# A Flamingo-style block on one core: the first half of batch 0 in two quarters of 256 tokens, with 25 split pieces of W0 held on chip

## The chip, the core and the metric

The kernel runs on one core of one Trainium2 chip. The metric is device time in microseconds (us), from the program's first instruction to its last with the launch around it, as a median of several runs. Five engines work side by side and meet through semaphores: TensorE (PE, matrix products and transposes), VectorE (DVE), ScalarE (ACT), GpSimd (POOL) and SyncE (SP), which issues most of the transfers between DRAM and the on-chip memory. Each engine takes its instructions strictly in the order of the program, so an instruction that waits holds back everything behind it on its engine.

## The reference

The input x has 4 batches of 1024 tokens with 1024 channels; ctx_2048, of the same shape, is the value v.

```
x = x + tanh(g_xattn) * wkv(w, u, k = layernorm(x), v = ctx_2048)
x = x + tanh(g_ffn)   * ffn(layernorm(x))

wkv: along the tokens, for each channel:  y = (p + e^(u+k) v) / (q + e^(u+k))
     p = e^w p + e^k v ;  q = e^w q + e^k        (written with running maxima)
ffn: D = gelu(f16(x) @ W0.T + b0) -> f16   (4096 columns)
     E = D @ W1.T + b1            -> f16   (1024 columns)
```

## The kernel before

**Work.** W0 and W1 are kept as two f16 parts (hi and lo), so each product is done twice and accumulated. W0 comes in 32 pieces of 128 rows. For a piece, `hi_piece` (ACT, two passes over 128x1024) writes the hi part and the scaled f32 piece, and `lo_piece` (POOL) writes the lo part; `store_piece` puts both into DRAM, from where later halves and batches read them back as blocks of four pieces (`load_parts`). All this is done once, in batch 0.

**Slots.** PE's main loop counts slots: a slot is one group of 16 products of 128 columns of weights with 512 tokens (8 blocks of channels, hi and lo). Per batch there are 64 slots of the first layer (`group1`, 32 pieces for each half of 512 tokens), then 64 of the second (`quarter2`). In batch 0 the first half of the tokens takes slots 0 to 31, and the second half 32 to 63. Each group accumulates in one of three banks (`BANKS`), which ACT empties with a Gelu (`gelu`); a group may start when the Gelu of three groups earlier is done.

**The front.** What a half needs before its first group is called the front here. For tiles of 128 tokens: the first layernorm (`stats_x`, `norm_x`, `lessen_x`: DVE and ACT, rstd on POOL), then, for each of 8 blocks of 128 channels, a *unit*: PE transposes the block (`unit`), ACT takes its exponential (`exps`), DVE runs seven operations (a product with v, two scans along the tokens, two fused operations, a reciprocal and a last fused one), and POOL adds the result to x (`residual`) and then sets the scan seeds of the unit after the next (`seed`). After all 8 units PE transposes back to tokens (`tokens_x2`), DVE does the second layernorm (`stats_x2`, `norm_x2`), PE transposes to channels (`channels_x2`) and ACT copies into XT (`copy_xt`), which is the moving operand of the first layer. The same steps serve the second half of batch 0; for batches 1 to 3 another form is used (`keys`, `means`, `variances`), which the change leaves as it is.

**Order.** The front of the first half stands ahead of the slots. All else is placed in the slots by hand: `UNIT_SLOT` says in which slot a unit starts, `LN1_SLOT` and `LN2_SLOT` do the same for the two layernorms. Exponentials and Gelus use different tables of ACT, so each unit inside the first layer's slots costs two table loads. In the fronts of batch 0 the units of the second half stand in slots 5 to 22, its second layernorm in slots 27 to 32, one tile per slot, and the 24 remaining pieces of W0 are split in slots 0 to 23.

Of the kernel before, what the change touches and what calls it, by code (L numbers as in the profile page):

```python
# [6 lines left out]
ALU = mybir.AluOpType  # L7
# [4 lines left out]
P = 128  # L12
# [19 lines left out]

UNIT_SLOT = {}
LN1_SLOT = {}
LN2_SLOT = {}
MEAN_SLOT = {}
VAR_AFTER, DEV_AFTER, SCALE_AFTER = 6, 8, 11
KEY_SLOT = {}


def place_front():
    for i, k in enumerate((5, 6, 9, 12, 14, 17, 20, 22)):
        UNIT_SLOT[CB + i] = k
    for i, k in enumerate((40, 43, 47, 50, 54, 57, 61, 64, 68, 71, 75, 78, 82, 85, 89, 92)):
        UNIT_SLOT[UNITS + i] = k
    for i in range(HT):
        LN1_SLOT[HT + i] = 1 + i
        LN1_SLOT[2 * HT + i] = 26 + 2 * i
        LN1_SLOT[3 * HT + i] = 52 + 2 * i
        LN2_SLOT[HT + i] = (27 + i, 29 + i)  # L50
    for h in range(2):
        MEAN_SLOT[2 + h] = 98 + 13 * h
    for i in range(HT):
        LN1_SLOT[2 * TILES + i] = 112 + 2 * i
    for b in (1, 2):
        at, n, T = SLOTS * b, UNITS * (b + 1), TILES * (b + 1)
# [8 lines left out]
    for n in range(UNITS, UNITS * B):  # L65
        KEY_SLOT[n] = UNIT_SLOT[n] - 2 if n % UNITS == 0 else UNIT_SLOT[n - 1]


place_front()
UNITS_AT = {k: [n for n in UNIT_SLOT if UNIT_SLOT[n] == k] for k in set(UNIT_SLOT.values())}  # L70
KEYS_AT = {k: [n for n in KEY_SLOT if KEY_SLOT[n] == k] for k in set(KEY_SLOT.values())}
LN1_AT = {k: T for T, k in LN1_SLOT.items()}
X2T_AT = {k[0]: T for T, k in LN2_SLOT.items()}
X2_AT = {k[1]: T for T, k in LN2_SLOT.items()}
# [6 lines left out]

def group_of(b, k):

    if k < GROUPS1:
        return GROUPS * b + k
    return GROUPS * b + GROUPS1 + (k - GROUPS1) // Q if k % Q == Q - 1 else None
# [10 lines left out]
def build(nc, x, xT, vT, consts, wrow, w0, w1, out):  # L97
# [6 lines left out]
    with ExitStack() as ctx:  # L104
# [35 lines left out]
        squares = xh[:, :].bitcast(F32)  # L140
        tokens = sb("tokens", [P, 2, HT])

        V = sb("V", [P, 2, HALF])
        S = sb("S", [P, 2, 2, HALF + 1])
# [8 lines left out]
        xo = sb("xo", [P, 2, L])  # L153
        ring = [stage[:, i, :] for i in range(RING2)] + [xo[:, i, :] for i in range(2)]
# [8 lines left out]
        x_landed, v_landed, xT_landed = sems("x_landed", HT), sems("v_landed"), sems("xT_landed", 8)  # L163
        x2_stored, xo_landed, out_stored = sems("x2_stored"), sems("xo_landed"), sems("out_stored")
        wst_landed, w_landed, w_stored = sems("wst_landed", RING1), sems("w_landed"), sems("w_stored")
# [19 lines left out]
        def unit_banks(n):  # L185

            pair = front[n % 2]
            return pair[:, 0, :], pair[:, 1, :]

        def token_banks(T):  # L190

            if T in (0, 3):
                return accs[:, 0:2, :]
            return front[(T + 1) % 2 if T < HT else T % 2][:, :, :]

        def last_stage_of(b):
            return GROUPS * (b + 1)
# [7 lines left out]
        def _(sp):  # L205
            def load_x(T):
                half, slot = T // HT, T % HT if T < TILES else T % 2
                if 0 < half < 4:
                    sp.wait_ge(kt_done, CB * min(half, 2))
# [9 lines left out]
            def load_norms(half):  # L219
# [3 lines left out]
                if half >= 4:  # L223
                    sp.wait_ge(k_ready, CB * (half - 3))
                row = norms_dram[half:half + 1].rearrange("o a p k -> o (a p k)")
                sp.dma_start(xin[:, 2 + half % 2, :], row.to_broadcast([P, 2 * HALF])).then_inc(norms_landed[half % 2], 16)

            def load_v(n):
                if n >= 2:
                    sp.wait_ge(ev_done, n - 1)  # L230
                sp.dma_start(V[:, n % 2, :], vT[n // UNITS, n % UNITS]).then_inc(v_landed[n % 2], 16)

            def load_xT(n):
                b, i = divmod(n, UNITS)
                if n >= 8:
                    sp.wait_ge(x2_done, n - 7)
                if b:

                    if b == 1:
                        sp.wait_ge(x2t_done, HT * (i // CB + 1))  # L240
                    else:
                        sp.wait_ge(scaled, UNITS * (b - 2) + CB * (i // CB + 1))
# [771 lines left out]
```

## Time and profile before

| what | us |
|---|---|
| median of 3 runs (1917.05 to 1918.54) | 1918.29 |
| the profiled execution | 1916.53 |
| its span, first to last instruction | 1914.7 |
| PE busy in the span | 1812.3 |
| DVE, ACT, POOL busy | 879.1, 555.7, 333.9 |

The span is what the trace shows; the profiled execution's time is 1.83 us longer than its span. PE busy counts from the start of a product to its modelled end. All stretches below are us from the span's start.

### The profile page before, as it was taken

The numbers are of one execution on the slowest core, as the hardware profiler recorded it, in microseconds if no ns is written. First come the engines' busy times: TensorE is split into PE (matmuls) and PEld (weight loads), VectorE is DVE, ScalarE is ACT, GpSimd is POOL, SyncE is SP. The second block draws the span as 40 slices with busy tenths as digits, with TensorE's granted clock in tenths as the row PEclk, the third lists the DMA queues.
The fourth block names the chain that finished last, engine by engine and source line by source line (L and its number), as shares of the span: only waits on it lengthen the run. The fifth ranks groups of instructions, "written<-read, shape, count | busy, mean of one in ns | idle before, by whom it ended". The sixth has DMA issues, their size and how long they took to land.

```text
span 1914.7 us, 20205 instructions
## 1 busy us (share of the span) xinstructions
PE 1812.3 (95%) x8408; PEld 829.5 (43%) x8408; DVE 879.1 (46%) x997; ACT 555.7 (29%) x673; POOL 333.9 (17%) x325
## 2 busy tenths in 40 slices
PE   1189899999999999999999999999999999999999
PEld 0144444444444444444444444444444444444444
DVE  8968748898447857633215867742300000000000
ACT  5059534634424434311003434410101221100000
POOL 4336402565211211200001221200000000000000
PEclk9999999999999999999999999999999999999999
DMA  6639776767574443332452443233233212222330
GB/s 247 247 118 327 236 259 232 251 238 267 195 213 143 146 151 133 141 108 104 138 185 106 149 160 137 89 132 128 93 120 132 88 45 88 88 81 95 132 121 34
DMA packets 82953, 291.89 MB, mean 152 GB/s; under 512 B 12583, under 2 KB 12583, under 8 KB 75693
## 3 DMA queue, kind: packets, MB, share of 16 engines
q1 hardware_dynamic: 74940, 177.30, 27.3%
q10 hardware_dynamic: 7920, 113.30, 16.8%
q8 instruction: 66, 1.08, 0.2%
q14 instruction: 27, 0.21, 0.0%
HBM read 223.41 MB, written 67.16 MB: 152 GB/s over the span
## 4 chain that ended last, share of the span: by engine, by line
PE 90%; DVE 1%; ACT 1%; DMA 1%; POOL 1%; issue 1%; SPq 0%; ACTq 0%; DVEq 0%; POOLq 0%
PE accs L903 45%; PE accs L925 44%; POOL W L447 0%; DVE stats L626 0%; DMA var_dram<-tokens 0%; ACT W L555 0%; PE front L861 0%; PE back L870 0%; DMA total<-var_dram 0%; PE front L884 0%; DVE XT L757 0%; PE front L879 0%; DVE xh L673 0%; DMA var_dram<-total 0%; PE front L837 0%
## 5 line engine op out<-in xcount | busy, mean ns | idle before, releaser
L903 PE MATMUL accs<-XT,W 128*128 128x512 f16 x4096 | 888.9, 379 | 4.2 <-ACT XT L527 2.4
L925 PE MATMUL accs<-DT,W 128*128 128x512 f16 x4096 | 886.7, 379 | 0.0
L925 PEld LDWEIGHTS accs<-DT,W 128*128 128x128 f16 x4096 | 400.8, 98 | 487.3 <-issue 6.8
L903 PEld LDWEIGHTS accs<-XT,W 128*128 128x128 f16 x4096 | 400.8, 98 | 486.3 <-issue 5.1
L765 DVE SCALAR_TENSOR_TENSOR xo<-e,tg,xo 128x512 f32<-128x512 f16 x64 | 50.3, 787 | 633.0 <-ACT e L572 633.0
L564 ACT ACTIVATE DT<-accs,small 128x512 f16<-128x512 f32 x256 | 175.6, 686 | 516.0 <-PE accs L903 515.4
L572 ACT ACTIVATE e<-accs,small 128x512 f16<-128x512 f32 x64 | 43.9, 686 | 660.3 <-PE accs L925 660.3
L720 DVE RECIPROCAL S<-front 128x512 f32<-128x512 f32 x64 | 214.4, 3350 | 0.0
L425 POOL TENSOR_TENSOR X<-X,S 128x512 f32<-128x512 f32 x64 | 92.5, 1446 | 521.1 <-DVE S L723 521.1
L447 POOL TENSOR_TENSOR W<-stage,W 128x1024 f16<-128x1024 f32 x52 | 110.6, 2138 | 46.3 <-ACT stage L558 46.3
L706 DVE TENSOR_TENSOR front<-front,V 128x512 f32<-128x512 f32 x64 | 44.5, 696 | 137.6 <-ACT front L522 136.0
L708 DVE TENSOR_TENSOR_SCAN S<-decay,S,front 128x512 f32<-128x512 f32 x64 | 81.3, 1271 | 0.0
L711 DVE TENSOR_TENSOR_SCAN S<-decay,S,front 128x512 f32<-128x512 f32 x64 | 80.4, 1256 | 0.0
L837 PE MATMUL front<-ident,xin 128*128 128x128 f32 x64 | 14.3, 355 | 61.6 <-DVE S L723 42.5
L555 ACT ACTIVATE W<-stage 128x1024 f16<-128x1024 f32 x52 | 54.5, 1048 | 46.3 <-DMA stage<-w_in 46.3
L757 DVE TENSOR_TENSOR XT<-X,total 128x512 f16<-128x512 f32 x48 | 30.0, 686 | 73.2 <-DMA total<-var_dram 73.2
L564 ACT ACT_TABLE_LOAD x49 | 62.9, 1283 | 0.9
L522 ACT ACT_TABLE_LOAD x48 | 61.6, 1283 | 0.8
L694 DVE TENSOR_TENSOR front<-X,xin 128x512 f32<-128x512 f32 x48 | 40.7, 847 | 42.0 <-DMA xin<-norms_dram 41.1
L558 ACT ACTIVATE stage<-stage 128x1024 f32<-128x1024 f32 x52 | 55.0, 1057 | 1.6
L522 ACT ACTIVATE front<-front,shift 128x512 f32<-128x512 f32 x64 | 42.3, 660 | 40.8 <-PE front L837 31.5
L723 DVE SCALAR_TENSOR_TENSOR S<-front,tg,S 128x512 f32<-128x512 f32 x64 | 48.1, 752 | 7.0 <-DVE S L720 0.5
(69 smaller groups left out, 596.1 us busy)
## 6 DMA issues: line engine op xcount, KB each, us to landing
W<-parts_dram ACTq DMA_DIRECT2D x54, 2048.0 KB, 9.2
parts_dram<-W SPq DMA_DIRECT2D x64, 512.0 KB, 5.1
stage<-w_in SPq DMA_DIRECT2D x52, 512.0 KB, 5.7
xin<-x_in SPq DMA_DIRECT2D x32, 512.0 KB, 7.0
V<-vT_in SPq DMA_DIRECT2D x64, 256.0 KB, 5.5
X<-xT_in SPq DMA_DIRECT2D x64, 256.0 KB, 6.6
x_dram<-X SPq DMA_DIRECT2D x32, 512.0 KB, 4.5
xo<-x_dram SPq DMA_DIRECT2D x32, 512.0 KB, 4.3
```

Of the source, the lines that this page charges most:

```text
L425: nc.gpsimd.tensor_tensor(slot, slot, S[:, n % 2, 1, 0:HALF], ALU.add).then_inc(x2_done, 1)
L447: nc.gpsimd.tensor_tensor(W[:, (g // Q) % 2, 1, g % Q, :], ring[ring_slot(g)[0]], W[:, (g // Q) % 2, 0, g % Q, :], ALU.subtract).then_inc( ...
L522: nc.scalar.activation(bank, bank, ACT.Exp, bias=shift[:, half, n % CB:n % CB + 1]).then_inc(e_ready, 1)
L555: nc.scalar.activation(W[:, s % 2, 0, g % Q, :], ring[slot], ACT.Copy, scale=W_SCALE)\
L558: nc.scalar.activation(ring[slot], ring[slot], ACT.Copy, scale=W_SCALE).then_inc(ws_done, 1)
L564: nc.scalar.activation(DT[:, nb, HALF * half:HALF * (half + 1)], acc[m % BANKS], ACT.Gelu, bias=b0[:, nb:nb + 1], scale=1.0 / W_SCALE).the ...
L708: nc.vector.tensor_tensor_scan(S_q[:, 1:], decay[:, c:c + 1].to_broadcast([P, HALF]), E, S_q[:, 0:1], ALU.mult, ALU.add).then_inc(q_done, 1)
L711: nc.vector.tensor_tensor_scan(S_p[:, 1:], decay[:, c:c + 1].to_broadcast([P, HALF]), EV, S_p[:, 0:1], ALU.mult, ALU.add).then_inc(p_done, 1)
L720: nc.vector.reciprocal(S_q[:, 0:HALF], E).then_inc(rec_done, 1)
L765: nc.vector.scalar_tensor_tensor(o, e16[:, half, :], tg[:, 1:2], o, ALU.mult, ALU.add)\
L903: mm = nc.tensor.matmul(acc[m % BANKS], W[:, (nb // Q) % 2, part, nb % Q, P * c:P * (c + 1)], XT[:, c, HALF * half:HALF * (half + 1)], sta ...
L925: mm = nc.tensor.matmul(acc[m % BANKS], W[:, s % 2, part, q, P * c:P * (c + 1)], DT[:, nb, HALF * half:HALF * (half + 1)], start=(nb == 0 ...
```

## The change

The first half of batch 0 is no longer prepared as 512 tokens, but as two quarters of 256. The front of the first quarter (8 units of 256 tokens, two tiles) stands ahead of the slots. Then follow 64 *early* groups of 16 products with 256 tokens (`group_early`, in the order of the table `EARLY`), two for each of the 32 pieces, so that the slots of batch 0 count 32 more (`EXTRA`). In early slots 0 to 24 (`LAG` = 25) the first quarter meets pieces 0 to 24, while the units of the second quarter run (in slots 1, 3, 8 and 13, two at a time). At slot 25 (`SECOND`) the second quarter's second layernorm and the first layernorm of the second half stand, with no group between them. From there the second quarter meets all pieces and the first quarter the last seven, while the second half's units (512 tokens) run from slot 31 to 61. At slot 64 (`THIRD`) the second half's second layernorm stands for all four tiles, again with no group between, and then slot 32 of the old count follows, unchanged.

Both quarters need each piece, so pieces 0 to 24 stay on chip until the second quarter has used them: `piece` places them in parts of X2, XT, DT and W that are not yet in use. 15 pieces are split ahead of the slots instead of 8, 10 more in early slots 1 to 19, the last seven in slots 34 to 52. Stores to DRAM start at early slot 3, each as two transfers. The second layernorm writes to two buffers in turn (`xhs`) instead of one. The units of batch 1 stand in slots 43 to 92 instead of 40 to 92 of the old count.

```diff
+LAG = 25
+EARLY = ([(0, nb) for nb in range(LAG)] + [(1, nb) for nb in range(12)] +
+         [x for j in range(NB - LAG) for x in ((0, LAG + j), (1, 12 + 2 * j), (1, 13 + 2 * j))] +
+         [(1, nb) for nb in range(12 + 2 * (NB - LAG), NB)])
+EXTRA = len(EARLY) - NB
...
+SECOND, THIRD = LAG, len(EARLY)
...
-    for i, k in enumerate((5, 6, 9, 12, 14, 17, 20, 22)):
-        UNIT_SLOT[CB + i] = k
+    for i, (k, a) in enumerate(((1, 5), (1, 8), (3, 10), (3, 13), (8, 16), (8, 19), (13, 21), (13, 24))):
+        UNIT_SLOT[CB + i], ADD_SLOT[CB + i] = k, a
+    for i, (k, a) in enumerate(((31, 36), (32, 41), (37, 46), (42, 50), (47, 55), (51, 60), (56, 63), (61, 63))):
+        UNIT_SLOT[2 * CB + i], ADD_SLOT[2 * CB + i] = k, a
...
+WITH_UNIT = ((0, 1), (2,), (3, 4), (5,), (6, 7), (8,), (9, 10), (11,))
+BEHIND = (12, 13, 14)
+PREP_SLOT = {15 + j: 1 + 2 * j for j in range(LAG - 15)}
+PREP_SLOT.update({LAG + j: 34 + 3 * j for j in range(NB - LAG)})
...
+            def group_early(m):
+
+                quarter, nb = EARLY[m]
+                pe.wait_ge(lo_done, nb + 1)
+                if m >= BANKS:
+                    pe.wait_ge(acc_drained, m - BANKS + 1)
+                for c in range(CB):
+                    for part in range(2):
+                        mm = nc.tensor.matmul(acc[m % BANKS][:, 0:QUARTER], piece_block(nb, part, c),
+                                              XT[:, c, QUARTER * quarter:QUARTER * (quarter + 1)],
+                                              start=(c == 0 and part == 0), stop=(c == CB - 1 and part == 1))
+                mm.then_inc(mm_done, 1)
...
-            for T in range(HT):
-                copy_xt(T)
+            hi_piece(BEHIND[0])
+            norm_x(2)
+            copy_xt(0)
+            copy_xt(1)
+            norm_x(3)
+            for g in BEHIND[1:]:
+                hi_piece(g)
...
+                    if K == SECOND:
+                        tokens_x2(2)
+                        tokens_x2(3)
+                        channels_x2(2)
+                        channels_x2(3)
+                    if K == THIRD:
+                        tokens_x2(4)
+                        for T in range(4, 8):
+                            if T < 7:
+                                tokens_x2(T + 1)
+                            channels_x2(T)
```

The names in the rows below leave out buffer numbers (front, X for X2); `xN` is the number of instructions that a row stands for. On PE, from the last transposes of the first front on, the order before was this (L903 the groups of 512 tokens, L837 a unit's transposes):

```order
L861 MATMUL accs<-ident,X 128x128 x8
L870 MATMUL back<-ident,xh 128x128 x16
L903 MATMUL accs<-XT,W 128x512 x80
L837 MATMUL front<-ident,xin 128x128 x4
L903 MATMUL accs<-XT,W 128x512 x16
L837 MATMUL front<-ident,xin 128x128 x4
L903 MATMUL accs<-XT,W 128x512 x48
```

and at the same place it is now this (L1083 the groups of 256 tokens, L1019 the transposes of two units):

```order
L1058 MATMUL back<-ident,xh 128x128 x8
L1058 MATMUL back<-ident,total 128x128 x8
L1083 MATMUL accs<-XT,X 128x256 x16
L1019 MATMUL front<-ident,xin 128x128 x4
L1083 MATMUL accs<-XT,X 128x256 x32
L1019 MATMUL front<-ident,xin 128x128 x4
L1083 MATMUL accs<-XT,X 128x256 x16
```

The groups begin after two tiles instead of four, and the next units' transposes stand one group behind the first instead of five. On ACT, the order from there on was this before (L527 the copies to XT, L564 Gelus and their table, L555 and L558 the two passes of a piece):

```order
L527 ACTIVATE XT<-back 128x8x128 x4
L564 ACT_TABLE_LOAD
L564 ACTIVATE DT<-accs,small 128x512
L555 ACTIVATE W<-xo 128x1024
L558 ACTIVATE xo<-xo 128x1024
L564 ACTIVATE DT<-accs,small 128x512
```

and is this now (L662 the copies, L638 a tile of the first layernorm, L694 and L696 a piece, L704 Gelus, L653 exponentials):

```order
L662 ACTIVATE XT<-back 128x8x128 x2
L638 ACTIVATE xin<-xin,offset,rstd 128x1024
L694 ACTIVATE W<-xo 128x1024
L696 ACTIVATE xo<-xo 128x1024
L694 ACTIVATE W<-xo 128x1024
L696 ACTIVATE xo<-xo 128x1024
L704 ACT_TABLE_LOAD
L704 ACTIVATE DT<-accs,small 128x256
L653 ACT_TABLE_LOAD
L653 ACTIVATE front<-front,shift 128x256 x2
L704 ACT_TABLE_LOAD
L704 ACTIVATE DT<-accs,small 128x256
```

A tile, two pieces, three table loads and a Gelu now stand between the last copy and the second Gelu, with the second quarter's first two exponentials among them. On POOL, at the first residuals in the slots, the order was this before (L447 `lo_piece`, L425 `residual`, L410 `seed`):

```order
L447 TENSOR_TENSOR W<-stage,W 128x1024 x3
L447 TENSOR_TENSOR W<-xo,W 128x1024 x2
L425 TENSOR_TENSOR X<-X,S 128x512
L410 COPY S<-state 128x2
L447 TENSOR_TENSOR W<-stage,W 128x1024
L425 TENSOR_TENSOR X<-X,S 128x512
L410 COPY S<-state 128x2
```

and is this now (L568 `lo_piece`, L544 `residual`, L528 `seed`):

```order
L568 TENSOR_TENSOR DT<-stage,DT 128x2x512
L544 TENSOR_TENSOR X<-X,S 128x256
L559 COPY state<-S 128x2
L528 COPY S<-state 128x2
L568 TENSOR_TENSOR DT<-stage,DT 128x2x512
L568 TENSOR_TENSOR DT<-xo,DT 128x2x512
L544 TENSOR_TENSOR X<-X,S 128x256
L559 COPY state<-S 128x2
L528 COPY S<-state 128x2
```

A residual, and the seed behind it, stands behind one or two pieces, as before, but the unit that waits for the seed is now half as long.

## Rows read from the trace of the kernel before

**Rows 1.** Busy time (instructions) by engine in three stretches; then clock, DMA, GB/s.

```profile
0.00:112.13 112.13, 22.05 (x96) 14.41 (x97) 93.64 (x113) 32.08 (x37) 37.41 (x55) 0.98 0.59 211
112.13:240.16 128.03, 121.95 (x608) 59.24 (x609) 100.99 (x112) 99.33 (x109) 70.01 (x53) 0.99 0.75 256
240.16:1914.70 1674.54, 1668.34 (x7704) 755.87 (x7704) 684.42 (x774) 424.34 (x528) 226.49 (x218) 1.00 0.41 141
```

**Rows 2.** Timeline, first front: start, length, engine, line [idle before].

```profile
14.37 0.69 PE L837 MATMUL front<-ident,xin 128*128 128x128 f32 x2 [2.19 <-DVE xin L660]
...
21.09 0.69 PE L837 MATMUL front<-ident,xin 128*128 128x128 f32 x2 [2.56 <-DVE xin L660]
...
22.39 0.70 DVE L706 TENSOR_TENSOR front<-front,V 128x512 f32<-128x512 f32 x1 [1.36 <-ACT front L522]
...
30.78 0.69 DVE L706 TENSOR_TENSOR front<-front,V 128x512 f32<-128x512 f32 x1
...
88.78 0.75 DVE L723 SCALAR_TENSOR_TENSOR S<-front,tg,S 128x512 f32<-128x512 f32 x1
```

**Rows 3.** Groups by line, shapes apart: busy us, mean ns, idle before; DVE, units.

```profile
L720 DVE RECIPROCAL S<-front 128x512 f32<-128x512 f32 x64 | 214.4, 3350 | 0.0
...
L708 DVE TENSOR_TENSOR_SCAN S<-decay,S,front 128x512 f32<-128x512 f32 x64 | 81.3, 1271 | 0.0
...
L723 DVE SCALAR_TENSOR_TENSOR S<-front,tg,S 128x512 f32<-128x512 f32 x64 | 48.1, 752 | 7.0 <-DVE S L720 0.5
...
L781 DVE SCALAR_TENSOR_TENSOR shift<-wp,shift 128x8 f32<-128x8 f32 x1 | 0.2, 168 | 0.0
```

**Rows 4.** Timeline, second layernorm of the first half, to the first group.

```profile
91.44 1.30 DVE L626 BATCH_NORM_STATS2 stats<-accs 128x6 f32<-128x512 f32 x2 [1.91 <-PE accs L944]
...
93.15 1.30 DVE L626 BATCH_NORM_STATS2 stats<-front 128x6 f32<-128x512 f32 x2
...
94.79 1.34 DVE L673 TENSOR_SCALAR xh<-accs,mv,rstd 128x1024 f16<-128x1024 f32 x1
...
96.18 1.03 PE L870 MATMUL back<-ident,xh 128*128 128x128 f16 x8 [3.08 <-DVE xh L673]
...
97.01 1.91 PE L861 MATMUL front<-ident,X 128*128 128x128 f32 x8
97.25 1.02 ACT L527 ACTIVATE XT<-back 128x1024 f16<-128x1024 f16 x1 [22.61 <-PE back L870]
...
112.13 1.46 PE L903 MATMUL accs<-XT,W 128*128 128x512 f16 x3 [1.11 <-ACT XT L527]
```

**Rows 5.** Groups by line, shapes apart: ACT and POOL.

```profile
L564 ACT ACTIVATE DT<-accs,small 128x512 f16<-128x512 f32 x256 | 175.6, 686 | 516.0 <-PE accs L903 515.4
L447 POOL TENSOR_TENSOR W<-stage,W 128x1024 f16<-128x1024 f32 x52 | 110.6, 2138 | 46.3 <-ACT stage L558 46.3
...
L564 ACT ACT_TABLE_LOAD x49 | 62.9, 1283 | 0.9
...
L555 ACT ACTIVATE W<-stage 128x1024 f16<-128x1024 f32 x52 | 54.5, 1048 | 46.3 <-DMA stage<-w_in 46.3
...
L522 ACT ACTIVATE front<-front,shift 128x512 f32<-128x512 f32 x64 | 42.3, 660 | 40.8 <-PE front L837 31.5 <-DVE front L698 8.8
```

**Rows 6.** Busy time in three short stretches, columns as in Rows 1.

```profile
113.00:114.00 1.00, 1.00 (x4) 0.42 (x3) 0.93 (x4) 0.38 (x1) 0.70 (x1) 0.50 0.00 0
116.00:117.00 1.00, 1.00 (x7) 0.43 (x5) 0.93 (x4) 0.00 (x0) 0.00 (x0) 1.00 0.00 0
200.00:206.00 6.00, 4.63 (x22) 1.89 (x20) 5.75 (x5) 5.91 (x8) 5.02 (x4) 1.00 0.51 197
```

**Rows 7.** Timeline, the end of the second half's last unit.

```profile
211.85 0.75 DVE L723 SCALAR_TENSOR_TENSOR S<-front,tg,S 128x512 f32<-128x512 f32 x1
```

**Rows 8.** The chain that ended last, from slot 32 on: start, length, what.

```profile
240.16 110.68 PE accs L903 x512
```

**Rows 9.** Busy time in a stretch of batch 1's units, columns as in Rows 1.

```profile
350.00:380.00 30.00, 30.00 (x140) 13.58 (x139) 20.70 (x20) 16.28 (x18) 19.63 (x15) 1.00 0.93 330
```

More of the change, by code:

```diff
@@ new lines, in _ @@
+            for g in BEHIND:
+                load_piece(g + RING1)
+            for b in range(B):
+                for k in range(0 if b else -EXTRA, SLOTS):
+                    K = EXTRA + SLOTS * b + k
+                    if K - 1 in PREP_AT and PREP_AT[K - 1] + RING1 < NB:
+                        load_piece(PREP_AT[K - 1] + RING1)
+                    if K in STORE_AT:
+                        store_piece(STORE_AT[K])
+                    if b == 0:
+                        if k == NB - Q + 1:
+                            for g in range(Q):
+                                stored(sp, g)
+                                stored(sp, LAG + g)
+                            load_parts(0, AT[1, LAG + Q - 1] + 1)
@@ L423, in residual @@
                 pool.wait_ge(xT_landed[n % 8], 16 * (n // 8 + 1))
-                slot = X2[:, n % UNITS, :]
-                nc.gpsimd.tensor_tensor(slot, slot, S[:, n % 2, 1, 0:HALF], ALU.add).then_inc(x2_done, 1)
-                half, c = n // CB, n % CB
-                if n >= UNITS and c:
+                b, h, off, w, c = chunk(n)
+                slot = X2[:, CB * h + c, off:off + w]
+                nc.gpsimd.tensor_tensor(slot, slot, S[:, n % 2, 1, 0:w], ALU.add).then_inc(x2_done, 1)
+                half = 2 * b + h
+                if n >= FIRST and c:
                     pool.wait_ge(x2_done, n + 1)
@@ L573, in round_e @@
                                      bias=b1[:, g // 2:g // 2 + 1], scale=1.0 / W_SCALE).then_inc(acc_drained, 1)
-            for T in range(HT):
+            for T in range(2):
                 norm_x(T)
@@ L783, in _ @@
             offset_x(0)
-            for T in range(HT):
-                if T + 1 < HT:
-                    stats_x(T + 1)
-                lessen_x(T)
-                if T + 1 < HT:
-                    offset_x(T + 1)
+            stats_x(1)
+            lessen_x(0)
+            offset_x(1)
+            lessen_x(1)
             dve.wait_ge(s_act0, 3)
@@ L857, in tokens_x2 @@
-                pe.wait_ge(y_done, UNITS * b + (UNITS if b else CB * (h + 1)))
-                if T >= 2:
-                    pe.wait_ge(xh_ready, T - 1)
+                ready = (2 if T < HT else 3) * CB
+                pe.wait_ge(x2_done, ready)
+                pe.wait_ge(y_done, ready)
+                pe.wait_ge(xh_ready, T - 1)
                 for c in range(CB):
-                    mm = nc.tensor.transpose(rows[:, c // HT, P * (c % HT):P * (c % HT + 1)],
-                                             X2[:, CB * h + c, P * (tile % HT):P * (tile % HT + 1)], ident[:, :])
+                    mm = token_piece(T, c)
```

522 lines of the change are left out of this document (320 added, 202 removed).

## The prediction

> **What bounds the kernel now.** The first view to read is busy time by stretch [rows 1]. From 240.16 to the end PE is busy 1668 of 1675 us: nothing can be won there except by fewer products, and the change has as many as before. From 112.13 to 240.16, the 32 slots of the first half, PE is busy 122 of 128. Before 112.13 it is busy 22, all of it transposes, while DVE is busy 94: the first front is one chain on DVE. So the time to win is the 112 us before the first group and the 6 us after. Whatever the change does is settled when slot 32 starts, at 240.16 [rows 8]; what follows keeps its 1674.5 us if nothing later is disturbed. I therefore work out when slot 32 starts.
>
> The timeline of the first front [rows 2] shows the first unit on DVE from 22.39, the second from 30.78, 8.39 later, and the eighth ending at 88.78 + 0.75 = 89.53: eight units without a gap. The second layernorm then takes 22.6 to the first group at 112.13 [rows 4]. In the second half the last unit ends at 211.85 + 0.75 = 212.60 [rows 7], and slot 32 comes 27.6 later.
>
> **The change, step by step.** Times are us from the span's start.
>
> *First unit.* Its transposes wait for tile 1 instead of tile 3: 14.37 instead of 21.09 [rows 2]. The exponential and DVE follow as before, 1.30 later, less about 0.25 for half the columns: 15.4 (before 22.39).
>
> *Eight units of 256 tokens.* Halving 8.39 gives 4.19, the lower bound. Seven operations each keep half of a fixed part; an operation on 8 columns takes 0.168, so the upper bound is 4.19 + 7 × 0.084 = 4.78. The longest, reciprocal (3.35) and scans (1.27) [rows 3], are nearly all columns, and neighbours overlap a little; I take 4.51. Eight units: 36.1, to 51.5 (before 89.53). ACT splits 1.5 pieces a unit, 1.5 × 2 × 1.05 = 3.1 plus the exponential [rows 5], and POOL 1.5 × 2.14 = 3.2 plus the residual: both fit below 4.51, so I add nothing; if loads of pieces come late, this cover is gone and up to 5 us are lost.
>
> *Second layernorm of two tiles.* DVE does three statistics of 1.64 (93.15 to 94.79), a normalization of 1.34, another statistic and normalization: 9.2, and 0.3 until POOL's last residual; then transposes 1.03 and copy 1.02, gaps 0.2 [rows 4]. The sum, 11.8, puts the first group at 63.3 (before 112.13): 48.8 won so far.
>
> *Slots 0 to 24.* PE: a group of 512 tokens takes 110.68/512 × 16 = 3.46 [rows 8], one of 256 between 1.73 and 1.75, since a product takes 216.2 ns where its columns at 2.4 GHz take 213.3; 25 groups are 43.8. The 32 transposes of units cost 2.4 (half of the 1.91 for eight, which were slow) [rows 4]. At the first group PE's granted clock was 0.50, that is 1.2 GHz, and it was 1.00 by 116 [rows 6]: 1.7 lost. Together 47.9.
> ACT: the rest of the first layernorm, one pass (about 1.2); twelve pieces of 2.1 (two for `BEHIND`, ten in the slots); nine table loads of 1.283; 25 Gelus and 8 exponentials of 256 columns. Those lie between half of 0.686 and all of it; by the difference between passes of 1024 (1.05) and 512 columns (0.66) [rows 5] a half-width one takes 0.47, and 0.40 with the overlap of neighbours. Sum: 1.2 + 25.2 + 11.5 + 13.2 = 51.1, with bounds 49.2 and 60.7. So ACT, not PE, sets this stretch. It ends the last piece before its last five Gelus, at 63.3 + 49.1 = 112.4, and PE has then about 5.9 of groups to go: 118.3.
> DVE: the second quarter's first exponential stands behind the pass, two pieces, two table loads, a Gelu and itself: 63.3 + 8.8 = 72.1. Eight units would end at 108.2. But each unit's scan needs a seed, which POOL writes behind the residual two units earlier, behind pieces that wait for ACT. For unit 10: piece 16 leaves ACT at 82.5 and POOL 2.14 later, residual and seed take 1.0, so 85.6, where DVE is ready at 81.5: it waits 4.1. The same sum for the next units gives 1 to 3 each and 9.4 in all: 117.6, and 118.4 with the last residual. Both chains meet at 118.3; I take that.
>
> *Slot 25.* PE has nothing but transposes until XT is there: eight transposes 0.95, two statistics 3.3, normalization 1.34, a first-layernorm pass taken at 0.8 (between half and all of that normalization, which has the same size), statistic 1.64, normalization 1.34, transposes and copy 2.05, less some overlap: 11.2. It is 129.5. Before, no such hole was there: the first half had one front.
>
> *To the second half's units.* Six groups (10.5) hide the rest of the first layernorm on DVE. Then Gelu, table load, exponential: 0.40 + 1.28 + 0.66 + 0.1. PE's clock may have fallen in the hole; I add half of 1.7. The first unit starts at 143.3. Eight units at 8.39, DVE-bound: 67.1, to 210.4. PE comes to the units' slots one to three us after the bank is free, and ACT needs three more, inside the 8.39; before, ACT was busy 99 of 128 in slots 0 to 31 [rows 1] with 24 pieces among them; here seven stand in this stretch.
>
> *Slot 64.* From the last unit to the first statistic 1.91 passed before (89.53 to 91.44), with one transpose left; now eight are left, 1.67 more. Four tiles then took 20.7 to the first group (91.44 to 112.13) [rows 4]; the second buffer takes out one wait, 0.45. So 210.4 + 3.6 + 20.2 = 234.2, and the clock has fallen again: 1.7 more, 235.9. Before, five groups of PE lay beside this chain; here none is left to put there.
>
> *Afterwards.* Batch 1's units begin three slots (10.4) later and end in the same slot. DVE idled 9.3 in 350 to 380 alone [rows 9], which takes up most of it: 0, at worst some 5. Transfers: SP issues each store as two and starts them later, behind waits for pieces; DMA was busy 0.75 of the time in slots 0 to 31 and 0.59 before [rows 1], and the same bytes are spread over the same stretch: 0. What stands behind those waits on SP are the loads of v for the second quarter's last units; they are issued some 8 us before their unit, which covers them.
>
> **Sum.** Slot 32 moves from 240.16 to 235.9: 4.3 won, out of 48.8 won at the first group. The span becomes 1910.4, the profiled execution (1.83 above its span) 1912.2, and the median, which was 1.76 above the profiled execution, **1914.0**.
>
> **Rivals.** A difference of 0.2%, 3.8 us, is about what can be told from no change here.
> (a) *Forecast*, 1914.0, own range 1910 to 1918: chance 0.46.
> (b) *The waits are not there.* If Gelus stay near their lower bound and POOL's pieces come in time, slots 0 to 24 end with PE, at 63.3 + 47.9 = 111.2, 7.1 earlier; units of 4.19 give 2.6 more: 1904.3. For it: both chains have bounds that low. Against it: the piece, table loads and Gelus on ACT are in strict order. Chance 0.19.
> (c) *All is given back*: the change brings the first group forward, but not slot 32. Gelus of 0.55 instead of 0.40 add 0.15 × 33 = 5.0 to ACT's stretch: 1919. For it: 48.8 won and 44.5 lost are both sums of estimates, so their difference can vanish. Chance 0.16.
> (d) *Slower, by the seeds.* The units of the second quarter wait for POOL, POOL for ACT's pieces, ACT for PE's groups between them. If the six gated units wait twice what I found, 18.8 instead of 9.4, slot 25 comes 9.4 later: 1923.4. It decides from 17.5 us of waits on. For it: ACT was busy 5.9 of 6 us at 200 to 206, where PE had gaps [rows 6], so such a loop exists. Against it: pieces come on ACT every 4 us, and a unit takes 4.5. Chance 0.12.
> (e) *Slower, by the clock.* If the gaps between groups in slots 0 to 24 take the clock to 1.2 GHz, 25 groups take 86.5 instead of 43.8, and with the transposes the stretch ends at 154.6, 36.3 later: 1950. Against it: from 200 to 206 PE was busy 4.63 of 6 and the granted clock stayed 1.00 [rows 6]; I expect 43.8 + 2.4 of 55 busy, about that share. Chance 0.07.
> The Trainium skill, "TensorE: Matmul & The Clock Gate", section "A second HAM failure mode: psum-queue depth-cycling", speaks for (e): it tells of a kernel that went round its PSUM banks and idled briefly between groups, so that its clock fell and rose again and again. By that rule the result would be somewhere between (a) and (e); no row here shows it yet.
>
> **The numbers.** The likeliest is (a), 1914.0. The range reaches down to (b) and up past (d), **1903 to 1925**; outside lie (e) and the tails of (b) and (d). Faster by over 0.2% (below 1914.5): all of (b) and over two thirds of (a), 0.52. Within 0.2%: the rest of (a) and most of (c), 0.28. Slower: (d), (e) and the tail of (c), 0.20.
>
> **What would show it.** In the changed kernel's profile: the first unit on DVE at 15.4, and eight in 36; the first group at 63 with the clock at 0.50; PE in gaps up to slot 18, released by ACT's Gelus, and DVE's scans waiting for seeds; slot 25's hole of 11 from about 118; the second half's first unit at 143 and eight in 67 without waits; slot 64's hole from the last unit's end near 210 for 24 us; slot 32's groups from 234 to 236. The prediction is wrong if slots 0 to 24 take under 50 or over 62 us, if the second half's units wait for ACT or PE, or if PE waits at batch 1's means.

## The result, and the profile after

The changed kernel takes **1929.11 us** (median of 7 runs, 1924.20 to 1931.39), the kernel before 1918.29 (7 runs, 1917.05 to 1919.52). The ratio is 1.0051, 95% interval 1.0038 to 1.0064: slower by half a per cent, clear of its interval, where 1914.0 was forecast. The profiled execution took 1929.11, its span 1927.3.

Busy time by stretch, columns as in [rows 1]. The second and the fourth row are the groups of 256 tokens, the third and the fifth the two pauses between fronts, the last begins at slot 32:

```profile
0.00:64.14 64.14, 13.05 (x49) 6.18 (x49) 55.12 (x95) 36.84 (x43) 40.14 (x57) 1.00 0.68 234
64.14:119.60 55.46, 48.33 (x416) 41.06 (x416) 38.36 (x59) 49.81 (x67) 31.53 (x33) 1.00 0.78 253
119.60:132.31 12.71, 4.03 (x32) 3.27 (x33) 12.07 (x23) 2.51 (x3) 3.17 (x7) 0.73 1.04 395
132.31:215.40 83.09, 74.77 (x656) 64.68 (x656) 69.54 (x66) 56.66 (x77) 27.16 (x23) 0.98 0.64 216
215.40:244.53 29.13, 10.79 (x64) 9.18 (x65) 19.61 (x30) 4.57 (x5) 4.19 (x7) 0.60 0.37 149
244.53:1927.30 1682.77, 1673.48 (x7704) 757.05 (x7704) 687.47 (x785) 424.48 (x528) 228.81 (x222) 1.00 0.41 140
```

The first group starts at 64.14 (before 112.13 [rows 4]), but slot 32 at 244.53 (before 240.16 [rows 8]), and the rest takes 1682.8, 8.2 more than before [rows 1]. So 4.4 us are lost ahead of slot 32 and 8.2 behind it. What is new stands in column PEclk, the granted clock (third from the right): 0.73 and 0.60 in the pauses. Its 1.00 in the first row is no reading, since this trace's first record of the clock is at 67.4. The transposes just ahead of the first group, and that group itself, ran at half clock: eight transposes took 1.03, where run 10 has 0.61 at full clock, and 16 products 3.48, where a later group took 1.91.

```profile
59.12 1.03 PE L1058 MATMUL back<-ident,xh 128*128 128x128 f16 x8 [4.62 <-DVE xh L831]
...
64.14 3.48 PE L1083 MATMUL accs<-XT,X 128*128 128x256 f16 x16 [1.12 <-ACT XT L662]
...
82.10 1.91 PE L1083 MATMUL accs<-XT,DT 128*128 128x256 f16 x16 [2.00 <-ACT DT L704]
```

```profile
118.95 0.61 PE L1060 MATMUL back<-ident,xh 128*128 128x128 f16 x8
```

VectorE's timeline (start, length, then in brackets the idle time ahead and what ended it): the first unit of each front, the unit of the second half that waits longest, and the last unit's last operation.

```profile
73.60 0.43 DVE L870 TENSOR_TENSOR front<-front,V 128x256 f32<-128x256 f32 x1 [6.40 <-ACT front L653]
...
147.16 0.70 DVE L870 TENSOR_TENSOR front<-front,V 128x512 f32<-128x512 f32 x1 [5.68 <-ACT front L653]
...
184.97 0.70 DVE L870 TENSOR_TENSOR front<-front,V 128x512 f32<-128x512 f32 x1 [3.94 <-ACT front L653]
...
219.99 0.75 DVE L887 SCALAR_TENSOR_TENSOR S<-front,tg,S 128x512 f32<-128x512 f32 x1
```

The second half's eight units take 147.16 to 220.74, 73.6, where eight without a wait take 67.1. Whom TensorE waited for between the pauses (total in us, times, longest):

```profile
PE accs L1083 <- POOL W L568: 8.0, 7, 1.9
PE accs L1083 <- ACT XT L662: 1.1, 1, 1.1
PE accs L1083 <- ACT DT L704: 0.3, 1, 0.3
```

Seven waits, one for the lower part of each of the pieces 25 to 31. TensorE's timeline behind the second pause:

```profile
244.53 112.52 PE L1102 MATMUL accs<-XT,W 128*128 128x512 f16 x512 [1.12 <-ACT XT L662]
356.89 117.58 PE L1124 MATMUL accs<-DT,W 128*128 128x512 f16 x544
476.45 1.53 PE L1067 MATMUL front<-total,share 128*128 128x512 f32 x2 [1.99 <-DVE S L887]
477.77 22.18 PE L1124 MATMUL accs<-DT,W 128*128 128x512 f16 x96
...
549.25 2.08 PE L1072 MATMUL front<-xh,share 128*128 128x512 f32 x2 [2.68 <-DVE xh L908]
```

Slot 32's 512 products take 112.52 (before 110.68 [rows 8]), the means of batch 1 wait 1.99 for its last unit, and the 96 products behind them take 22.18; the same count at the second means, further on, takes 20.88. From 477 to 480 the granted clock was 0.50. Why batch 1 comes late stands in VectorE's and ScalarE's rows:

```profile
281.16 0.76 DVE L857 SCALAR_TENSOR_TENSOR front<-grow,wp,front 128x512 f32<-128x512 f32 x1
287.33 0.70 DVE L870 TENSOR_TENSOR front<-front,V 128x512 f32<-128x512 f32 x1 [5.42 <-ACT front L653]
...
285.27 1.28 ACT L653 ACT_TABLE_LOAD   x1
286.57 0.66 ACT L653 ACTIVATE front<-front,shift 128x512 f32<-128x512 f32 x1
...
368.33 1.06 ACT L694 ACTIVATE W<-stage 128x1024 f16<-128x1024 f32 x1 [4.52 <-DMA stage<-w_in]
```

VectorE has its keys at 281.92 and waits for the exponential of the first unit, which stands in slot 43.

### The profile page after: what moved, and what is told of

Its sections match the earlier page's. It is cut to its first block, busy times and chain, and to the rows that moved or that the text cites. A ratio compares the mean times of both kernels' runs of the same rounds, so it can differ in the third digit from the quotient of the medians.

```text
span 1927.3 us, 21556 instructions
## 1 busy us (share of the span) xinstructions
PE 1824.5 (95%) x8920; PEld 881.4 (46%) x8920; DVE 882.2 (46%) x1053; ACT 574.9 (30%) x721; POOL 335.0 (17%) x349
## 4 chain that ended last, share of the span: by engine, by line
PE 77%; DVE 11%; ACT 4%; issue 4%; POOL 3%; DMA 1%; SPq 0%; DVEq 0%; POOLq 0%; ACTq 0%
PE accs L1124 38%; PE accs L1102 36%; DVE S L884 3%; PE accs L1083 1%; POOL W L568 1%; DVE S L872 1%; DVE S L875 1%; DVE stats L784 1%; POOL X L544 1%; DVE front L870 1%; ACT L653 1%; DVE front L853 1%; DVE front L881 1%; DVE front L878 1%; ACT L704 1%
## 5 line engine op out<-in xcount | busy, mean ns | idle before, releaser
L1102 PE MATMUL accs<-XT,W 128*128 128x512 f16 x3584 | 776.0, 380 | 1.1 <-ACT XT L662 1.1
L712 ACT ACTIVATE DT<-accs,small 128x512 f16<-128x512 f32 x224 | 154.0, 688 | 490.9 <-PE accs L1102 490.4
L884 DVE RECIPROCAL S<-front 128x512 f32<-128x512 f32 (+1 forms) x72 | 215.6, 2994 | 0.0
L544 POOL TENSOR_TENSOR X<-X,S 128x512 f32<-128x512 f32 (+1 forms) x72 | 94.0, 1305 | 492.6 <-DVE S L887 492.6
L870 DVE TENSOR_TENSOR front<-front,V 128x512 f32<-128x512 f32 (+1 forms) x72 | 45.8, 636 | 135.1 <-ACT front L653 135.1
L568 POOL TENSOR_TENSOR W<-stage,W 128x1024 f16<-128x1024 f32 x41 | 86.7, 2128 | 60.3 <-ACT stage L696 60.3
L872 DVE TENSOR_TENSOR_SCAN S<-decay,S,front 128x512 f32<-128x512 f32 (+1 forms) x72 | 83.0, 1153 | 8.7 <-POOL S L528 8.7
L875 DVE TENSOR_TENSOR_SCAN S<-decay,S,front 128x512 f32<-128x512 f32 (+1 forms) x72 | 81.9, 1138 | 0.0
L1083 PE MATMUL accs<-XT,W 128*128 128x256 f16 x480 | 54.9, 273 | 9.8 <-POOL W L568 8.0
L694 ACT ACTIVATE W<-stage 128x1024 f16<-128x1024 f32 x41 | 43.0, 1048 | 51.6 <-DMA stage<-w_in 51.6
L696 ACT ACTIVATE stage<-stage 128x1024 f32<-128x1024 f32 x52 | 55.0, 1057 | 1.6
L784 DVE BATCH_NORM_STATS2 stats<-xin 128x6 f32<-128x512 f32 x64 | 41.0, 683 | 30.3 <-DMA xin<-x_in 30.3
L1083 PEld LDWEIGHTS accs<-XT,W 128*128 128x128 f16 x480 | 46.3, 98 | 17.4 <-POOL W L568 9.8
L887 DVE SCALAR_TENSOR_TENSOR S<-front,tg,S 128x512 f32<-128x512 f32 (+1 forms) x72 | 49.8, 692 | 7.5
```

What stands on the lines that cost most here:

```text
L544: nc.gpsimd.tensor_tensor(slot, slot, S[:, n % 2, 1, 0:w], ALU.add).then_inc(x2_done, 1)
L568: nc.gpsimd.tensor_tensor(lo, staged, hi, ALU.subtract).then_inc(lo_done, 1)
L712: nc.scalar.activation(DT[:, nb, HALF * half:HALF * (half + 1)], acc[m % BANKS], ACT.Gelu, bias=b0[:, nb:nb + 1], scale=1.0 / W_SCALE).the ...
L784: nc.vector.bn_stats(stats[:, i, h, :], halves[h]).then_inc(bn_done[i], 1)
L870: nc.vector.tensor_tensor(EV, E, values, ALU.mult).then_inc(ev_done, 1)
L872: nc.vector.tensor_tensor_scan(S_q[:, 1:w + 1], decay[:, c:c + 1].to_broadcast([P, w]), E, S_q[:, 0:1], ALU.mult, ALU.add).then_inc(q_done, 1)
```

## The experiments

Medians are given with the ratio to the kernel before, run beside it on the same chip; differences between kernels are differences of these ratios times 1918.3 us. All versions lie within 1% of the kernel before, so where two intervals meet, a difference rests on the traces as well. Edits are to the changed kernel unless another run is named; `...` stands for code that is not shown.

**1. The last seven pieces earlier.**

```
-PREP_SLOT.update({LAG + j: 34 + 3 * j for j in range(NB - LAG)})
+PREP_SLOT.update({LAG + j: 33 + 2 * j for j in range(NB - LAG)})
```

> Only the slots of ScalarE's and GpSimd's work on the last seven pieces of W0 (25 to 31) move: 33, 35, 37, ... in place of 34, 37, 40, ... so three to nine groups stand between a piece's slot and its use, in place of two. Theory (the pieces' loop): between the Gelu of a piece's slot and its first use ScalarE needs 1.05 and 1.06 us and GpSimd 2.12 us, more than the two groups of 1.75 us behind which they are hidden, so TensorE waits for nearly every piece (8.0 us in all), the exps behind its stalled stream come late, and VectorE's units lose 6 us (waits of 3.94, 1.28, 0.70 and 0.16). Expected: these waits are gone, the last unit ends near 214 in place of 220.7, slot 32 starts near 238 in place of 244.5, and the kernel takes 6 to 7 us less than the changed kernel, about 1922.6, still slower than before. Rival (the stretch is VectorE's and ScalarE's own: the 3.94 comes from table loads and queues on ScalarE): TensorE's wait on GpSimd goes but the units' end stays within 2 us, and the time stays within 2 us of 1929.

1921.79, ratio 1.0017 (1.0008 to 1.0026): 6.5 us less than the changed kernel. The loop stands in the changed kernel's timelines, here ScalarE's, GpSimd's and TensorE's rows for one piece:

```profile
166.93 0.48 ACT L704 ACTIVATE DT<-accs,small 128x256 f16<-128x256 f32 x1 [3.38 <-PE accs L1083]
167.31 1.05 ACT L694 ACTIVATE W<-stage 128x1024 f16<-128x1024 f32 x1
168.38 1.06 ACT L696 ACTIVATE stage<-stage 128x1024 f32<-128x1024 f32 x1
...
169.52 2.13 POOL L568 TENSOR_TENSOR W<-stage,W 128x1024 f16<-128x1024 f32 x1 [4.60 <-ACT stage L696]
...
171.70 1.92 PE L1083 MATMUL accs<-XT,W 128*128 128x256 f16 x16 [0.88 <-POOL W L568]
```

The Gelu waits for TensorE, the piece's halves for the Gelu, GpSimd for them, and TensorE for GpSimd: 4.8 us round, with two groups (3.5) to cover it. With the edit one wait of 0.4 is left of the 8.0, and VectorE waits for ScalarE once in place of four times:

```profile
PE accs L1083 <- POOL W L568: 0.4, 1, 0.4
...
DVE front L870 <- ACT front L653: 6.6, 1, 6.6
```

The units take 148.57 to 216.34, 67.8, and slot 32 comes at 240.13 (expected 238: the first unit came 1.4 later than in the changed kernel). The theory holds. Of the 7.1 between the two profiled executions, 4.4 lie ahead of slot 32 and 2.7 behind it, where TensorE's wait at the second variances is 1.39 instead of 2.68 and the clock does not fall after it.

**2. The seeds earlier.**

```
-(1, 5), (1, 8), (3, 10), (3, 13), (8, 16), (8, 19), (13, 21), (13, 24)
+(1, 3), (1, 3), (3, 5), (3, 7), (8, 9), (8, 11), (13, 13), (13, 15)
```

> Only the residual additions of the second quarter's units stand earlier in GpSimd's order (slots 3, 3, 5, 7, 9, 11, 13, 15 in place of 5, 8, 10, 13, 16, 19, 21, 24), ahead of the lower parts of pieces they stood behind; the scan of the unit after next waits for each. Theory (TensorE and ScalarE set the first stretch): the four waits of VectorE for its seeds, 8.6 us, go and the second quarter's last unit ends near 111 in place of 119.8, but the 25 groups still end at 119.5, and the tokens' transposes stand behind them; only the wait of 1.1 us for GpSimd ahead of the tokens and the first norm's first statistics (1.7 us) come out of the path: 1 to 2.5 us less than the changed kernel. Rival (the seeds set the stretch, as the second of the prediction's rivals had it): 7 to 9 us less, near 1921.

1936.10, ratio 1.0088 (1.0074 to 1.0101): 7.1 us **more**: neither theory nor rival. The last residuals now stood ahead of pieces that TensorE wanted sooner, and GpSimd, with these pieces behind it, waited 6.1 for a unit that came late, since VectorE now waited for values (6.8 in two waits):

```profile
116.18 3.40 PE L1083 MATMUL accs<-XT,DT 128*128 128x256 f16 x16 [3.69 <-POOL DT L568]
```

The first quarter's 25 groups end at 126.8 in place of 119.5. This shows only that GpSimd's order is tight; run 9 asks the question again.

**3. The means one slot later.**

```
-MEAN_SLOT[2 + h] = at + 98 + 13 * h
+MEAN_SLOT[2 + h] = at + 99 + 13 * h
```

> Only the two products of the means of batch 1 and what hangs on them move one slot (3.45 us) later, 98 to 99 and 111 to 112. Theory (batch 1's units end too late for the old slot): TensorE's wait of 1.99 us at the first means and the half clock behind it (1.8 us by the rows) go, and the scaled halves are still done before batch 1's first group (7.4 us of slack now): 3 to 4 us less than the changed kernel, about 1925.5. Rival 1: only the wait goes, since the clock falls for another reason: 2 us less. Rival 2: the slack is used up and batch 1's first group waits, 0 or more.

1929.77, ratio 1.0058 (1.0044 to 1.0072): no gain. The wait at the means is gone, but two waits at the variances, which hang on the same slots, are 4.8 where there were 2.7:

```profile
501.05 1.13 PE L1072 MATMUL front<-xh,share 128*128 128x512 f32 x2 [0.58 <-DVE xh L908]
...
552.13 1.16 PE L1072 MATMUL front<-xh,share 128*128 128x512 f32 x2 [4.21 <-DVE xh L908]
```

Slot 32 also came 0.9 later in this execution (245.45), though nothing ahead of it had been changed. Moving the place of the wait gives nothing back; batch 1 itself has to come sooner (run 6).

**4. Unread products in the pauses.** `warm(K, n)` is n products of the identity and 256 columns into the bank that group K overwrites.

```
+warm(K, 32)
 channels_x2(2)
+warm(K, 20)
 channels_x2(3)
+warm(K, 8)
...
+warm(K, 56)
 tokens_x2(4)
 for T in range(4, 8):
     if T < 7:
         tokens_x2(T + 1)
+    warm(K, 24 if T < 7 else 8)
     channels_x2(T)
+warm(K, 8)
```

> TensorE does products that nobody reads (identity by 256 columns, 0.11 us each at the full clock) in the idle time of the two pauses in batch 0's first half: 60 in the first, 144 in the second, into the accumulator that the next group overwrites. The result is unchanged. Theory (the pauses let the clock fall): the granted clock stays near 1.00 through both, the four groups behind the first pause take 7.0 us in place of 8.8 and slot 32's first groups lose nothing (1.8 us now): 1.8 to 3.5 us less than the changed kernel, about 1926.5. Rival: the products themselves run at the half clock or stand in the way of the transposes, and the pauses grow by what the clock gains: within 1 us, or slower.

1920.12, ratio 1.0010 (1.0001 to 1.0019): 7.9 us less, more than twice what was expected. The stretch of the second pause, in the changed kernel and in this one:

```profile
215.00:245.00 30.00, 11.61 (x70) 9.45 (x68) 20.41 (x33) 4.57 (x5) 4.19 (x7) 0.60 0.38 152
```

```profile
215.00:245.00 30.00, 26.53 (x222) 20.12 (x221) 18.45 (x30) 4.78 (x5) 5.27 (x9) 1.00 0.41 150
```

Granted clock 0.60 against 1.00. The theory had priced the groups behind the pauses alone: the four behind the first (8.77 to 7.16) and slot 32's (1.8). What it missed is in the pause: its transposes are links of the chain.

```profile
222.14 3.67 PE L1040 MATMUL front<-ident,X 128*128 128x128 f32 x16 [6.78 <-POOL X L544]
...
229.73 1.91 PE L1040 MATMUL front<-ident,X 128*128 128x128 f32 x8
```

```profile
220.13 1.97 PE L1040 MATMUL front<-ident,X 128*128 128x128 f32 x16 [0.67 <-POOL X L544]
...
226.46 1.04 PE L1040 MATMUL front<-ident,X 128*128 128x128 f32 x8
...
238.74 6.43 PE L1109 MATMUL accs<-XT,W 128*128 128x512 f16 x29 [0.24 <-ACT XT L662]
```

From the tokens' transposes to slot 32 the changed kernel needs 22.4, this one 18.6: 3.8 us for the half clock, though TensorE also did 88 unread products in between. The profiled executions are 9.0 apart: 2.0 up to these transposes, 3.8 from there to slot 32, 1.8 in slot 32's products and 1.4 behind them. The kernel before had 1.00 there too: it laid groups beside the chain.

**5. Edits 1 and 4 together.**

> The edits of the pieces' run and of the run with unread products together. Theory (two separate causes: TensorE's waits for the late pieces, 7.3 us by the first run, and the half clock in the pauses, 9 us by the other): they add up, 15 to 16.5 us less than the changed kernel, 1912.5 to 1915, so less than before; slot 32 starts near 234 to 235. Rival (both gave back the same idle time of TensorE, once): no more than 10 us less, near 1919.

1913.09, ratio 0.9977 (0.9968 to 0.9986): 14.2 us less than the changed kernel, against 6.5 + 7.9 = 14.4 singly. The two causes are separate, and without them the change is a gain, though a small one. Slot 32 comes at 232.94, and 1677.5 follow it.

**6. Batch 1 as before**, on top of 5: its units back at slots 40, 43, 47, ..., the loads of its first x tiles at slot 33, ahead of the norms' load, and the last store of batch 0's x2 at slot 32.

```
-    for i, k in enumerate((43, 46, 49, 52, 56, 59, 62, 66, 69, 72, 76, 79, 82, 85, 89, 92)):
+    for i, k in enumerate((40, 43, 47, 50, 54, 57, 61, 64, 68, 71, 75, 78, 82, 85, 89, 92)):
...
-                    if K in (45, 54, 63, 67):
-                        store_x2({45: 17, 54: 19, 63: 21, 67: 23}[K])
+                    if K in (45, 54, 63, 64):
+                        store_x2({45: 17, 54: 19, 63: 21, 64: 23}[K])
...
-                    for n in UNITS_AT.get(K + 6, ()):
+                    for n in UNITS_AT.get(K + (6 if b else 7), ()):
```

> As the run with both edits, and batch 1's units back at the slots that they had before the change (first at 40, not 43), with the loads of their first x tiles issued ahead of the load of the norms (slot 33; the last store of batch 0's x2 moves to slot 32 for that). Theory (batch 1 starts late because its norms' load stands behind four x tiles that are issued 3 us ahead of it: 13.6 us from issue to landing, 4.8 before the change): the norms land near 5 us after their issue, the first unit starts 10 us earlier than now relative to slot 32, and TensorE's wait at the first means (2 to 3.3 us) and the clock it costs there (1.6) go: 3 to 5 us less than with both edits. Rival (the loads of the tiles of x behind the pause set it, waits of 5.55 and 5.28 us): the keys are late for slot 40, ScalarE holds the Gelus behind the exps and TensorE waits there: same time or slower.

1909.53, ratio 0.9960 (0.9947 to 0.9972): 3.3 us less than run 5. The first unit of batch 1 starts 31.7 behind slot 32 (run 5: 41.0, changed kernel 42.8), TensorE waits at no means, and from slot 32 to the end it is 1674.3 again, as before the change. The theory's reason does not hold: the norms took 8.7 from issue to landing, where run 5, with the old order of loads, had 5.8 (changed kernel 13.6). By the two traces VectorE starts on the first keys only 2.8 earlier than in run 5 (260.29 instead of 263.11), while the 6.4 that it then waited there for the exponential in slot 43 are gone. So the larger part comes from the units' slots. Three things were moved at once, and no run moved one alone.

**7. The first pause spread out**, on top of 6: residuals at slots 3, 3, 7, 9, 11, 13, 15, 17, the second half's units one slot earlier, and the transposes of the second quarter's second layernorm laid between the last groups, with 8 of run 4's 60 unread products left there:

```
+if K == SECOND - 4:
+    tokens_x2(2)
+    tokens_x2(3)
+if K == SECOND - 1:
+    channels_x2(2)
 if K == SECOND:
-    tokens_x2(2)
-    tokens_x2(3)
-    channels_x2(2)
     channels_x2(3)
+    warm(K, 8)
...
-if K == SECOND:
-    copy_xt(2)
-    copy_xt(3)
+if K in (SECOND - 1, SECOND):
+    copy_xt(3 - SECOND + K)
```

> As the run before it, and the first pause is spread out: the residuals of the second quarter's units stand at slots 3, 3, 7, 9, 11, 13, 15, 17, each ahead of the scan that needs it and behind the pieces that are wanted first; tokens 2 and 3 are transposed ahead of group 21 instead of behind group 24, the channels of tile 2 ahead of group 24, and the second half's units stand one slot earlier. Theory (VectorE's chain sets the end of the first half once TensorE's groups stand in the pause): its seed waits (8.6 us) go, the units end near 111, slot 25 starts near 125 in place of 132, the second half's first unit near 137 in place of 147, and slot 32 is reached 7 to 9 us earlier than in the run before it; the time falls by as much. Rival (ScalarE sets this stretch, hi parts and table loads): the units' exps come late, and 0 to 3 us are gained.

1904.05, ratio 0.9929 (0.9915 to 0.9942): 5.9 less than run 6; slot 32 at 226.93, 5.9 earlier. That is less than the 7 to 9; VectorE now waits 2.3 for values of the second quarter, which it did not before.

**8. Two exps ahead of the first Gelu**, on top of 7.

```
-for g in BEHIND[1:]:
-    hi_piece(g)
+hi_piece(BEHIND[1])
+exps(CB)
+exps(CB + 1)
+hi_piece(BEHIND[2])
...
-exps(n)
+if n >= CB + 2:
+    exps(n)
```

> As the run before it, and on ScalarE the first two exps of the second quarter stand ahead of piece 14's upper part and of the first Gelu (the Exp table is then loaded two times less in a row of Exp and Gelu). Theory (the 6.40 us that VectorE idles ahead of the second quarter's first unit are ScalarE's order): the first unit starts near 70 in place of 73.6, and all that follows on VectorE comes 2 to 4 us earlier, as does slot 32. Rival: TensorE's transposes for these two units come at 68 at the half clock and the first Gelu comes later, so TensorE's groups end later: within 1 us, or slower.

**1901.48**, ratio 0.9915 (0.9902 to 0.9929): 2.7 less than run 7, 16.3 less than the kernel before, and the fastest here. The unit starts at 68.73, but part of it is lost to a load:

```profile
68.73 0.43 DVE L872 TENSOR_TENSOR front<-front,V 128x256 f32<-128x256 f32 x1 [1.55 <-ACT front L653]
...
91.65 0.43 DVE L872 TENSOR_TENSOR front<-front,V 128x256 f32<-128x256 f32 x1 [4.26 <-DMA V<-vT_in]
```

**9. The seeds alone**, on the changed kernel, with run 7's residual slots.

> The changed kernel with only the residuals of the second quarter's units at slots 3, 3, 7, 9, 11, 13, 15, 17, so that each stands behind the piece that is wanted before it and ahead of the scan that needs it; the earlier try had put the last of them ahead of pieces and made TensorE wait. Theory (the 25 groups set the first stretch, not the seeds): the seed waits of 8.6 us go, the groups still end near 119.5, and 1 to 2.5 us are gained. Rival (the seeds set it): 7 to 9 us.

1927.25, ratio 1.0046 (1.0032 to 1.0060): 1.0 less, which the intervals do not tell from nothing. The seed waits are gone, and VectorE idles in their place for transposes that stand behind TensorE's 25 groups:

```profile
DVE stats L784 <- PE front L1040: 6.5, 1, 6.5
```

**10. Run 8 without the unread products.**

> The fastest version so far without its unread products. Theory (the half clock costs in the second pause itself, by slower transposes on the chain, and in the groups behind it): the granted clock falls to about 0.6 in the second pause, the pause grows by 3 to 4 us, slot 32's first groups lose 1.8 us, and since batch 1's means no longer wait nothing more is lost there: 5 to 6.5 us slower than the version with them, about 1907. Rival (the clock costs 9 us wherever it falls, as in the run with unread products alone): about 1910.5.

1909.16, ratio 0.9953 (0.9940 to 0.9965): 7.3 us slower than run 8, between theory and rival; its profiled execution is 6.5 longer. Columns as in [rows 1], from the end of the early groups in run 8 to slot 32:

```profile
199.58:229.63 30.05, 12.45 (x81) 10.43 (x78) 20.52 (x31) 4.99 (x6) 4.21 (x7) 0.66 0.60 233
```

The tokens' transposes to slot 32 take 22.4 again (run 8: 18.6), slot 32's products 112.73 (110.68), and 1.5 come from the first pause and the groups behind it, where a wait of 1.1 for XT was left (0.24 in run 8) and the clock was 0.88 from 119 to 133. The half clock costs this also where the other two causes are gone.

**11. Values earlier**, on top of 8: their loads at slots 2, 3, 5, 7, the tokens' transposes ahead of group 19 and those of tile 2's channels ahead of group 23.

> The fastest version with the loads of the values of units 12 to 15 issued at slots 2, 3, 5 and 7 (not 4, 7, 10, 12), ahead of the loads and stores of pieces there, and tokens 2 and 3 transposed ahead of group 19 (not 21), the channels of tile 2 ahead of group 23. Theory (VectorE's wait of 4.26 us for values there is on the path): the second quarter's units end near 106.5, the second half's first unit starts 3 to 4.5 us earlier, and the time falls by as much, to about 1897.5. Rival (TensorE's and ScalarE's 25 groups now set the first pause's end): 0 to 2 us.

1906.21, ratio 0.9936 (0.9924 to 0.9949): 4.0 **slower** than run 8 (its profiled execution, the fastest of five, is 2.4 longer, and slot 32 comes 2.8 later). The loads came in time, but the statistics now came before GpSimd was done with the pieces that stand ahead of them in its order, the last of which waited 5.71 for ScalarE's part:

```profile
119.84 1.34 DVE L833 TENSOR_SCALAR xh<-front,mv,rstd 128x1024 f16<-128x1024 f32 x1 [6.66 <-POOL rstd L535]
```

## Why the prediction was wrong, point by point

Forecast for the span was 1910.4; it was 1927.3. By the prediction's own steps, from the profiled execution:

| step | forecast | measured | adds |
|---|---|---|---|
| first unit; eight units of 256 | 15.4; 36.1 | 15.35; 37.2 | |
| first group | 63.3 | 64.14 | |
| slots 0 to 24 end | 118.3 | 119.5, tokens at 120.67 | |
| slot 25 | 129.5 | 132.31 | 2.8 in all so far |
| second half's first unit | 143.3 | 147.16 | 3.9 in all so far |
| its eight units | 67.1 | 73.6 | 6.5 |
| last unit to slot 32 | 23.8 | 23.8 | 0 |
| clock at slot 32 | 1.7 | 1.8 | 0.1 |
| afterwards | 0 | 6.4 | 6.4 |

The last entry on starts, 3.9, and the four below it make 16.9, the whole difference. Two of the signs that the prediction gave for its being wrong came true: the second half's units wait, and TensorE waits at batch 1's means.

- **The step that failed most** is "eight units at 8.39, DVE-bound: 67.1". ScalarE's three us per unit did fit, as written; that TensorE would wait for GpSimd's part of the "seven pieces" that stand there was not asked. Their slot comes three groups ahead of their use, and the way over ScalarE and GpSimd is longer than what lies between. The prediction priced pieces by engine time, never by the distance from slot to use. With the pieces earlier (run 1) the units take 67.8, and 6.5 come back in the whole.
- **"Afterwards: 0, at worst some 5"** failed too. 2.0 of wait at the means, 1.1 more at the second variances and 3.2 of half clock behind the two are nearly all of the 6.4. Batch 1's first unit starts 42.8 behind slot 32, before 30.6: the 12.2 are the three slots that were seen (10.4) and slot 32's half clock (1.8). VectorE's idle time [rows 9] took up only part of them: the eighth unit starts 130.8 behind slot 32, before 125.1. There VectorE waited 7.17 for an exponential, which stands on ScalarE behind a piece of weights whose load came late (4.52); from there to the means VectorE has no gap left to take up more. Run 6 shows that the loss can be had back.
- **The clock was in the sum only in part.** The prediction gave it 1.7 at slot 32 (measured 1.8) and half of that behind the first pause (measured 1.6), and nothing in batch 1, where it cost 3.2. That the second pause came out right, 23.8, was luck of the rows: the chain of [rows 4] was itself run at half clock, as the 1.91 for eight transposes shows (1.04 at full clock in run 4). So what the new pause cost against a chain with groups beside it was in the sum without a name. That it could be avoided was not seen: keeping the clock up is worth 7.9 (run 4) and 7.3 (run 10).
- **Slots 0 to 24 were right**: 55.4 against 55.0, set by ScalarE, whose last piece ends at 113.36 (forecast 112.4), with TensorE's six waits for Gelus (7.0 in all) and VectorE's seed waits of 8.6 (forecast 9.4). So rival (b), which had no waits, falls. Run 9 shows that the seeds hide behind the groups, so rival (d) falls: the slower side was right, its mechanism was not. Two slips in the working did not matter: TensorE has 16 transposes of units there, not 32 (four rows of 0.60 make the 2.4; 32 at its price would be 3.8), and ScalarE's upper bound adds up to 60.5, not 60.7.
- **Rival (e)**, half clock through that stretch, did not come: the changed kernel's trace has 1.00 there behind the first group. But runs 1 and 3, whose kernels are the same up to slot 25, and run 9 each show one short fall in it. In run 1 the clock was 0.65 from 84 to 88, behind a wait of 2.01, and 32 products took 5.42 where 3.65 is the rule; the row of 82.10 above is the same place in the changed kernel, where a wait of 2.00 was followed by full speed:

```profile
82.07 5.42 PE L1083 MATMUL accs<-XT,DT 128*128 128x256 f16 x32 [2.01 <-ACT DT L704]
```

  In run 1 the stretch ends at 120.06, in the changed kernel at 119.54. The Trainium skill, "TensorE: Matmul & The Clock Gate", section "A second HAM failure mode: psum-queue depth-cycling", tells of a clock that falls and rises again and again where TensorE goes round its PSUM banks and idles briefly between groups. These traces agree only in part: at most one fall came in 25 groups, and in one of the four traces none.
- Of the rivals, (c) came nearest in kind, all won is given back, but not by longer Gelus on ScalarE, as it had it (they took 0.47 each, not 0.55); the time went past its 1919 and past (d)'s 1923.4.

**Open**: how run 6's gain divides among its three moves; and why the changed kernel's own runs lie in two clusters (three from 1924.2 to 1926.4, four from 1929.1 to 1931.4). The falls of the clock differ from execution to execution of the same code, as slots 0 to 24 show, but that does not settle it: run 9, whose pauses fell as well, spans 1.7, run 8 0.4, and the kernel before, beside runs 1 to 4, 7.3.

## What to carry to other kernels

When work is moved to a slot ahead of its use, count the whole way from that slot to the use, over every engine it passes, against what lies between; busy shares don't show it. A schedule that brings the first product forward but leaves TensorE alone with a chain of transposes pays twice, in the chain and behind it: lay products beside such a chain, real ones where there are some, and unread ones where there are none. Moving one wait in a tight order mostly makes another (runs 2, 3 and 11), so read what stands behind the moved instruction before it is moved.

## What the runs showed of the hardware

- Pauses in which TensorE did only transposes, with waits of 1 to 7 us between, had a granted clock of 0.60 to 0.73 (the two levels are 1.2 and 2.4 GHz); with products in the same gaps it was 1.00 (run 4). TensorE was also idle for some two thirds of these pauses (busy 4.03 of 12.71 and 10.79 of 29.13), so no run here tells whether transposes alone would have kept the clock up.
- Eight transposes of 128x128 in f32 took 1.04 us at the full clock and 1.91 at half, in f16 0.62 and 1.03.
- A single wait of 1.99 us at the means was followed by 96 products in 22.18 us in place of 20.88. A wait of 2.24 at the second variances in run 8 was followed by full speed (176 products in 38.15, as in the kernel before), so the length of a wait alone did not decide it.
- Unread products, 204 of them and some 22 us of TensorE's time, gave back 7.9 us net.
